# Writing the sorted message rows of a two-layer graph network with an accumulating scatter into a zeroed array

## The reference, cut to what matters

```python
# layer 0: one message per edge, summed at the edge's src
h = silu(edge_rbf @ W1 + b1)
messages = node_feats[dst] * (h @ W2 + b2)            # (212500, 128)
aggregated = segment_sum(messages, src, 12500)
x1 = layernorm(x + concat(node_feats @ Wself + bself, aggregated) @ Wcat + bcat)

# layer 1: means over edges in both directions, then a GRU cell
a_in  = seg_mean((x1 @ W_in.T + b_in)[src],  dst)
a_out = seg_mean((x1 @ W_out.T + b_out)[dst], src)
out = layernorm(x1 + gru_cell(concat(a_in, a_out), x1, ...))
```

## Time and profile before

| | |
|---|---|
| Median of 3 runs | 8655.38 us (8653.27 to 8666.53) |
| Span of the profiled execution | 11114.2 us (no other time is given for it) |
| TensorE, VectorE, ScalarE, GpSimd busy | 5877.2, 4372.7, 1003.5, 5203.3 us |
| HBM read, written in the execution | 515.84 MB, 138.14 MB |

### The profile page before, as it was taken

One profiled execution on the slowest core, in us unless ns is written; L12 is line 12 of the kernel. 1 busy time (PEld: TensorE's weight loads), 2 busy tenths in 40 slices (PEclk: granted clock), 3 DMA queues, 4 the chain that ended last, 5 costly groups with the idle time before them and its releaser, 6 DMA issues.

```text
span 11114.2 us, 137603 instructions
## 1 busy us (share of the span) xinstructions
PE 5877.2 (53%) x29570; PEld 4978.3 (45%) x29570; DVE 4372.7 (39%) x15403; ACT 1003.5 (9%) x2201; POOL 5203.3 (47%) x5478
## 2 busy tenths in 40 slices
PE   5688888888887877782222222222222222222239
PEld 5466666666666667772222222222222222222224
DVE  4733333333333357644333333333333333333335
ACT  5211111111111100010000000000000000000004
POOL 0044445455445420005555555555555555555530
PEclk9766666666666678755555555555555555555569
DMA  1022222222222246521222211212422222222232
GB/s 36 30 69 68 70 69 71 69 69 74 69 68 73 68 122 178 175 88 39 41 42 41 42 41 41 42 41 41 38 42 41 41 42 40 42 41 41 42 42 78
DMA packets 954829, 668.08 MB, mean 60 GB/s; under 512 B 643694, under 2 KB 839395, under 8 KB 954134
## 3 DMA queue, kind: packets, MB, share of 16 engines
q0 software_dynamic: 170112, 360.70, 12.6%
q1 hardware_dynamic: 717853, 242.18, 9.4%
q10 hardware_dynamic: 66816, 64.65, 2.0%
HBM read 515.84 MB, written 138.14 MB: 59 GB/s over the span
## 4 chain that ended last, share of the span: by engine, by line
SPq 28%; issue 21%; PE 8%; DVEq 2%; DVE 1%; DMA 1%; ACTq 1%; another core or an unknown queue 1%; POOL 0%; ACT 0%; POOLq 0%
SPq L436 22%; SPq L290 4%; PE bank L1374 3%; DVEq L290 1%; DMA arena<-msgs 1%; SPq L291 1%; PE bank L1444 1%; ACTq L290 1%; PE bank L1403 1%; PE bank L1445 1%; PE bank L1446 1%; DVEq L1018 1%; PE bank L1393 1%; SPq L439 0%
## 5 line engine op out<-in xcount | busy, mean ns | idle before, releaser
L559 POOL DMA_INDIRECT arena<-x1d,arena x3520 | 3345.4, 950 | 2390.8 <-issue 1097.1
L1418 PE MATMUL bank<-arena 128*128 128x129 f32 x7040 | 1601.7, 419 | 4180.4 <-DVE arena L1139 1716.2
L1418 PEld LDWEIGHTS bank<-arena 128*128 128x128 f32 x7040 | 1491.0, 322 | 4291.3 <-issue 3955.6
L524 POOL DMA_INDIRECT msgs<-arena x1664 | 1748.6, 1051 | 2258.4 <-DVE arena L992 1781.1
L1323 PE MATMUL bank<-w2s,arena 128*128 128x128 f32 x3328 | 1036.5, 404 | 0.0
L1150 DVE TENSOR_TENSOR acc_b<-acc_b,bank 128x129 f32 x1760 | 510.9, 290 | 1275.7 <-remote 619.8
L1150 DVE TENSOR_TENSOR acc_a<-acc_a,bank 128x129 f32 x1760 | 510.9, 290 | 1157.0 <-remote 520.0
L1315 PE MATMUL bank<-arena,w1pad 64*128 64x128 f32 x3328 | 768.8, 400 | 363.3 <-issue 336.9
L1315 PEld LDWEIGHTS bank<-arena,w1pad 64*128 64x128 f32 x3328 | 657.3, 291 | 411.5 <-issue 385.6
L1343 PE MATMUL bank<-arena 128*128 (+1 forms) x3328 | 781.5, 410 | 0.0
L1139 DVE TENSOR_SCALAR arena<-iota_row,blk1d,arena 128x128 f32<-128x128 f32 x1760 | 496.6, 362 | 705.1 <-issue 703.8
(11 more groups left out here) (241 smaller groups left out, 4925.3 us busy)
## 6 DMA issues: line engine op xcount, KB each, us to landing
arena<-rows SPq DMA_DIRECT2D x208, 512.0 KB
arena<-msgs SPq DMA_DIRECT2D x464, 136.0 KB, 2.8
arena<-msgs ACTq DMA_DIRECT2D x464, 136.0 KB, 3.0
arena<-x1d,arena POOLq DMA_INDIRECT x3520
arena<-msgs SPq DMA_DIRECT2D x1760, 1.0 KB
arena<-dlist SPq DMA_DIRECT2D x1760, 1.0 KB
msgs<-arena POOLq DMA_INDIRECT x1664
arena<-xwin SPq DMA_DIRECT2D x208, 64.0 KB
```

Of the source, the lines that this page charges most:

```text
L524: pool.indirect_dma_start(msgs, bass.IndirectOffsetOnAxis(ap=pos[:, b, j:j + 1], axis=0), mrow[:, b, j, :], None).then_inc(scattered[b], 16)
L559: pool.indirect_dma_start(grow[:, sl, 0:D], None, x1d, bass.IndirectOffsetOnAxis(ap=edge2[:, sl, 1:2].bitcast(i32), axis=0)).then_inc(gath ...
L1418: last = mm(bank[q % 2 * 4 + k // 2][:, (k % 2) * 256:(k % 2) * 256 + CW], oh1[:, q % 2, k, :], grow[:, q * TG + k, :], start=True, stop=True)
```

## The change

Two things are changed together. The message array `msgs` is filled with zeros from SBUF, and the scatter of each message row then adds to what lies there. As an addition of floats is made on all 136 words of a row, the `dst` node can no longer lie there as an integer: ScalarE writes its value as a float, and in half 0 of the gather stage VectorE makes integers of it again, into a new buffer `edge_i`.

```diff
+        edge_i = cut(NS, i32)
...
+        ZR = P * 2 * TG                 # 2048 rows a DMA
+        NZ = EP // ZR                   # 104 DMAs
...
 @block.sync
+            sp.wait_ge(s["mrow_zero"], 1)
+            for c in range(NZ):
+                sp.dma_start(msgs[c * ZR:(c + 1) * ZR, :].rearrange("(p r) c -> p (r c)", p=P),
+                             mrow.rearrange("p b j c -> p (b j c)")).then_inc(s["zeroed"], 16)
             sp.wait_ge(s["prepared"], 1)
...
 scatters, GpSimd
-                        pool.indirect_dma_start(msgs, ...(ap=pos[:, b, j:j + 1], axis=0), mrow[:, b, j, :], None).then_inc(scattered[b], 16)
+                        pool.indirect_dma_start(msgs, ...(ap=pos[:, b, j:j + 1], axis=0), mrow[:, b, j, :], None, compute_op=ALU.add).then_inc(scattered[b], 16)
...
 gathers, GpSimd
-                        hold(pool, edge2_in[q], 16 * TG * (it + half * IT1 + 1))
+                        if half == 0:
+                            hold(pool, s["idx_ready"], it * 4 + q + 1)
+                        else:
+                            hold(pool, edge2_in[q], 16 * TG * (it + half * IT1 + 1))
                         for k in range(TG):
                             sl = q * TG + k
-                            pool.indirect_dma_start(grow[:, sl, 0:D], None, x1d, ...(ap=edge2[:, sl, 1:2].bitcast(i32), axis=0)).then_inc(gathered[q], 16)
+                            at = edge_i[:, sl:sl + 1] if half == 0 else edge2[:, sl, 1:2].bitcast(i32)
+                            pool.indirect_dma_start(grow[:, sl, 0:D], None, x1d, ...(ap=at, axis=0)).then_inc(gathered[q], 16)
...
 edge_group, ScalarE
-                    nc.scalar.activation(mrow[:, b, :, D + 1:D + 2].rearrange("p j c -> p (j c)").bitcast(i32), dst_idx[...], ACT.Copy)
+                    nc.scalar.activation(mrow[:, b, :, D + 1:D + 2].rearrange("p j c -> p (j c)"), dst_idx[...], ACT.Copy)
...
 end of the preparation, VectorE
-            st.link(v.memset(mrow[:, :, :, :], 0.0))
+            v.memset(mrow[:, :, :, :], 0.0).then_inc(s["mrow_zero"], 1)
+            dve.wait_ge(s["zeroed"], 16 * NZ)
             dve.sem_inc(s["prepared"], 1)
...
 onehots1, VectorE
                         dve.wait_ge(edge2_in[q], 16 * TG * (it + half * IT1 + 1))
+                        if half == 0:
+                            v.tensor_copy(edge_i[:, q * TG:(q + 1) * TG], edge2[:, q * TG:(q + 1) * TG, 1:2]...).then_inc(s["idx_ready"], 1)
                         need(dve, s["sum1_ready"], first + q - 1)
```

More of the change, by code:

```diff
@@ L263, in gnn_kernel @@
         grow_ones w1_in slow_pool lotab_out reg_done wide_in digits_read local_ready edges_below slow_blocks slow_counted
-        slow_hist limits rows_float columns_ready columns_read blk0_copied""".split()
+        slow_hist idx_ready mrow_zero zeroed limits rows_float columns_ready columns_read blk0_copied""".split()
         s = {n: sem(n) for n in names}
@@ L523, in scatters @@
                     for j in range(TG):
-                        pool.indirect_dma_start(msgs, bass.IndirectOffsetOnAxis(ap=pos[:, b, j:j + 1], axis=0), mrow[:, b, j, :], None).then_inc(scattered[b], 16)
+                        pool.indirect_dma_start(msgs, bass.IndirectOffsetOnAxis(ap=pos[:, b, j:j + 1], axis=0), mrow[:, b, j, :], None, compute_op=ALU.add).then_inc(scattered[b], 16)
             with pool.Fori(0, NG // 2) as it:
@@ L555, in _ @@
                     for q in range(4):
-                        hold(pool, edge2_in[q], 16 * TG * (it + half * IT1 + 1))
+                        if half == 0:
+                            hold(pool, s["idx_ready"], it * 4 + q + 1)
+                        else:
+                            hold(pool, edge2_in[q], 16 * TG * (it + half * IT1 + 1))
                         for k in range(TG):
                             sl = q * TG + k
-                            pool.indirect_dma_start(grow[:, sl, 0:D], None, x1d, bass.IndirectOffsetOnAxis(ap=edge2[:, sl, 1:2].bitcast(i32), axis=0)).then_inc(gathered[q], 16)
+                            at = edge_i[:, sl:sl + 1] if half == 0 else edge2[:, sl, 1:2].bitcast(i32)
+                            pool.indirect_dma_start(grow[:, sl, 0:D], None, x1d, bass.IndirectOffsetOnAxis(ap=at, axis=0)).then_inc(gathered[q], 16)
             y_rows = acc_b[:, 0:NB * CW].rearrange("p (n c) -> p n c", c=CW)
@@ L648, in edge_group @@
                     nc.scalar.activation(mrow[:, b, :, D:D + 1].rearrange("p j c -> p (j c)"), src_key[:, bass.ds(g * TG, TG)], ACT.Copy).then_inc(s["key_ready"], 1)
-                    nc.scalar.activation(mrow[:, b, :, D + 1:D + 2].rearrange("p j c -> p (j c)").bitcast(i32), dst_idx[:, bass.ds(g * TG, TG)], ACT.Copy).then_inc(s["key_ready"], 1)
+                    nc.scalar.activation(mrow[:, b, :, D + 1:D + 2].rearrange("p j c -> p (j c)"), dst_idx[:, bass.ds(g * TG, TG)], ACT.Copy).then_inc(s["key_ready"], 1)
                     if not (last and b):
@@ L1136, in onehots1 @@
                         dve.wait_ge(edge2_in[q], 16 * TG * (it + half * IT1 + 1))
+                        if half == 0:
+                            v.tensor_copy(edge_i[:, q * TG:(q + 1) * TG], edge2[:, q * TG:(q + 1) * TG, 1:2].rearrange("p s c -> p (s c)")).then_inc(s["idx_ready"], 1)
                         need(dve, s["sum1_ready"], first + q - 1)
```

## The result

The changed kernel takes **10,793.9 us** (median of 4, 10,779 to 10,799), before 8,661.0 us beside it: ratio 1.2464, 95% interval [1.2448, 1.2479]. That is 2,133 us more, where 1,356 us more were predicted, and above the range (9,300 to 10,750).

What follows compares the result with a forecast made beforehand. The prediction held the gather stage to be paced by GpSimd, at 0.95 to 1.25 us a gather. It summed 8,655 + 370 (fill) + 986 (index wait), with 0 for the scatter, to 10,011 us, range 9,300 to 10,750.

Steps and rivals of the forecast that it cites:

- "I take 0" for the scatter: Edge stage: the adding scatters cost 0 us more, covered by GpSimd's room in a group of 16.9 us.
- the threshold that I gave: Edge stage: a scatter must reach 1.71 us on GpSimd before the group gets longer.
- rival 2: Edge stage: adding scatters take twice as long, 2.10 us, and GpSimd becomes the bound; 645 us more, 10,656 us; chance 0.18.
- the placing of the 2,459 us: Difference between profile span and median, put down to the profiler holding up queues in stretches of the gather stage.
- The fill: Before the edge stage: zeroing 115.9 MB at 313 GB/s, covered by nothing, adds 370 us (202 to 549).
- The index wait: Gather stage, half 0: GpSimd waits for VectorE's index copy, 17.2 us at each of 54 turns; 986 us (782 to 1,250).
- Rival 1: Gather stage, half 0: SyncE sets the pace, so the index wait costs 0 to 340 us; 9,025 to 9,365 us; chance 0.12.
- Rival 3: Edge stage: the fill's pause frees TensorE's clock from 0.64 to 1.0, giving 1,100 us back; 8,539 us; chance 0.03.
- The rule on adds: Cited with rival 2: an add inside a DMA emits two read descriptors per piece instead of one and halves the rate.

Runs made afterwards that it cites:

- L8.7: The faster of two levels of time for the unchanged kernel, steady within a set of runs: 8,634 to 8,663 us.
- L11: The slower of two levels of time for the unchanged kernel, steady within a set of runs: 10,703 to 11,107 us.
- c0: The changed kernel run again, unaltered, in a set where before took 10,703 us: 11,713 us, ratio 1.0945.
- set a: Set of runs with before at 11,088 us; before plus the fill alone took 11,362 us, before plus the index detour alone 11,674 us.
- g1: The changed kernel with a copying scatter in place of the adding one, before at 8,634 us: 9,816 us, ratio 1.1364.
- the plain scatter: The changed kernel with a copying scatter in place of the adding one: 9,816 us where before took 8,634 us.
- the paced one: Before with a GpSimd memset that has no reader behind each copying scatter: 9,375 us, ratio 1.0823, where before took 8,663 us.
- the early fill: The changed kernel with the fill issued by GpSimd during preparation and the index copy on ScalarE: 10,893 us, ratio 0.9802; again 10,875 us, ratio 0.9859.
- set c: Set of runs with before at 10,703 us; the changed kernel with its index copy on ScalarE took 11,122 us, ratio 1.0400.

## Why the prediction was wrong, point by point

**The step that failed: "I take 0" for the scatter.** It rested on a group of 16.9 us with 6.1 us of room for GpSimd. At L8.7 the group has 11.2 us and GpSimd no room at all, so the threshold that I gave, 1.71 us a scatter, was in truth the 1.08 us that it had. The add brought it to 1.66 us, less than the doubling of rival 2, and cost 951 us, more than rival 2's 645. Rival 2 had the mechanism and the wrong base. At L11, the level of the trace that I read, the group indeed didn't get longer at 1.66 us (15.76 us in c0, against 16.7 to 16.9 in the traces of before); that it would get shorter I did not see.

**Under it lay the placing of the 2,459 us** between span and median. I put nearly all of it into the gather stage, with a gather at 0.95 us, and called it the profiler's. It was 1,272 us in the gather stage (5,767 to 4,495) and 1,174 in the edge stage (3,510 to 2,336), and spans and times of the same execution lie 1.6 to 1.7 us apart in every run, so the profiler had no part in it. The text named the right reading in passing (with the spacing of 0.30 us the gathers take 4,400 us "and other stages would have to shrink too") and passed it over, though the spacing stood in every row of GpSimd. With 4,400 us taken, 8,660 - 4,400 less the other stages would have left about 2,400 us for the edge stage, 11.6 us a group, against 10.8 us of GpSimd: the room would have been seen to be gone.

**The fill**: 370 us predicted, 278 measured in the L8.7 trace, 274 alone in set a. That nothing covers it was right. It ran at 408 GB/s with the DMA engines 98% busy, above every stretch of the earlier trace rows. The Trainium skill's page "DMA: Bandwidth & Descriptors", section "Bandwidth", has 425 GB/s for a 16 MB load, by which I had estimated 273 us; this trace agrees with it within 4%, and the rows of short mixed bursts that I preferred did not.

**The index wait**: 986 us predicted, 885 measured, and the 28 us ahead of the first gather, which the prediction left out. It was right in place and kind; the turn measures 16.3 us in the mean against 17.2, and inside an iteration, where 55 us were taken, almost nothing is waited beyond the spacing (0.36 us in the mean ahead of a quarter, with 0.30 of spacing in it). That its price shows in full only where GpSimd paces half 0 was right, and so was the lower price at L11 in kind (340 predicted, 586 to 616 measured).

**Rival 1** (index wait covered) fell: the wait is covered at neither level. **Rival 3** (TensorE's clock after the pause) fell: the clock reads 0.50 in the fill, and 0.68 in the edge stage behind it, below before's 0.86 at the same level. The clean comparison is g1, with the fill and without the add: 0.87, with the same 2,336 us for the stage, so the pause gives nothing back.

**The rule on adds** (the Trainium skill, "Collectives: The Full Stack", section "The bandwidth ceiling: the fold count and why AG ≠ RS ≠ AR"): a second read descriptor for each piece, there for the reducing step between cores. The traces show 0.6 us more per 128 rows on GpSimd, 1.6 times and not twice, and a DMA share of 0.52 in the edge stage in place of 0.32, far from full. What they show beside it is eight times the packets for a scatter and no more bytes: the pages count 360.70 MB in GpSimd's queue and 515.84 MB read from HBM with and without the add, so a read of the old rows shows in neither count. The packets of GpSimd's queue take 40.0% of the DMA engines' time in the edge stage in place of 14.1%. Whether GpSimd's extra time goes to more packets, to descriptors for a read, or to something else is not shown by any run.

**Open**: why the queues are held up in some sets, and why there a train of copying scatters 1.26 us apart stretches the edge stage to 16.9 us while slower ones don't. At L8.7 only the changed kernel, the plain scatter and the paced one ran, and all are slower than before; the index copy on ScalarE and the early fill were timed at L11 alone. If they did at L8.7 what they did there, all but the add's 951 us would go (an argument, not a run).

## What to carry to other kernels

Before pricing anything as covered, make the stages of the trace add up to the time that will be judged; where span and median differ by 28%, the cover read from the span may not exist. A copy that another engine waits for costs what stands ahead of it in its own engine's order: in set a 0.17 us of work, 220 times, cost 586 us on VectorE, and on the idle ScalarE (set c) the same work cost nothing that shows. And where GpSimd issues indirect DMAs back to back, what is added to one of them is paid in full: here 0.6 us on each of 1,664 came to 951 us.

## What the runs showed of the hardware that I had not expected

The same program takes 8,634 to 11,107 us from one set of runs to the next, steadily within a set, and the slower level shows in the queues: a register move of 29 ns takes up to 1,412. An adding indirect scatter of 128 rows of 544 bytes occupies GpSimd 1,551 ns in place of 958 (medians), at both levels, and goes out as 128 packets in place of 16. A copying one takes longer, up to 2,223 ns, where it falls under one VectorE instruction, L972 (256 of the 1,664 scatters, 254 of them under it). A fill of 115.9 MB from SBUF ran at 408 GB/s. And at the slower level idle work on GpSimd made the kernel 3.8% faster, TensorE's clock in the mean from 0.63 to 0.66.
